# A decoder layer on one core: when VectorE divides, and in which bank the contexts are turned

## The chip, the cores and the metric

The kernel runs on 1 core of one Trainium2 chip. The metric is the device time of one execution in microseconds (us), the median of several runs. The engines: PE (TensorE, matmuls and transposes into PSUM), DVE (VectorE), ACT (ScalarE), POOL (GpSimd) and SP (SyncE, which here issues DMAs). PSUM has 8 banks of 128 x 512 f32. Engines wait for each other by semaphores alone; the kernel is written without a scheduler.

## What is computed

Four sequences of 256 tokens, 128 wide, go through three residual blocks: a windowed local attention, a cross-attention on a context of 512 rows for each sequence, and a routed mixture of 12 experts with two weight matrices each. The change touches the cross-attention (16 heads of 64):

```python
lat = layer_norm(latents, ln_lat_g, ln_lat_b)
ctx = layer_norm(context, ln_ctx_g, ln_ctx_b)
q = lat @ Wq; k, v = split(ctx @ Wkv)          # by heads
k = apply_rope(k, cos, sin)
attn = clip(einsum('bhnd,bhsd->bhns', q, k) * scale, -11, 11)
out = einsum('bhns,bhsd->bhnd', softmax(attn), v)
x = x + out.reshape(b, n, INNER) @ Wo + bo
```

Products that need more than one pass are split: an operand is kept as a rounded part (`_hi`, made by ACT) and the rest (`_lo`, made by DVE as a subtraction), and three matmuls stand for one.

## The kernel before

The span has three stretches. Up to about 61 us the local attention runs, with the first keys, values and queries of the cross-attention in its gaps. Then come 32 rounds (`for r in range(NPAIR)`), one for each pair of heads, 8 for each sequence, up to about 277 us. The experts follow, first all `W1` products, then all `W2` products.

**A round.** Each engine has its own loop over r, in a fixed order, written out by hand. In PE's round r: `scores` of pair r+1 (line 1200, two halves of 8 matmuls each, into banks 0 to 3); `unit`, one tile of values for later rounds (lines 1005 to 1007, into bank 5, `EXTRA_BANK`); `key_products` of pair r+6 (lines 1016 to 1018, bank 6, `MISC_BANK`); in even rounds `queries` (lines 1134 to 1136) of two pairs to come, into the bank of an earlier pair's output; `weigh_values` of pair r (line 1219) and `sum_weights` (line 1229), both into bank 4 or 7. In rounds named in `extras` something stands at the end, in bank 5: in rounds 3, 12 and 17 the next sequence's latents are turned (line 1112), in rounds 11, 13, 19 and 21 a finished tile is projected by `Wo` (line 1238); the projections of rounds 27 and 29 go to bank 6. Values end with round 27, keys with round 25.

**Contexts.** The normalised context of sequences 1, 2 and 3 is turned by four transposes (`turn_context`, line 979) in rounds 0, 6 and 14, ahead of that round's value unit, into bank 6. ACT reads it twice (`context_f`, lines 718 and 724: an affine copy `ctx_f`, then `ctx_hi`), DVE makes `ctx_lo` (line 1491). The keys of the same round use bank 6 too, so they wait until ACT has read it (`misc_free`).

**DVE's round** begins with `divide(r - 1)`: the reciprocal of the denominators (line 1626) and the product `o_t` (line 1630). Then come, where due, a step of the latents' normalisation (`LATENT_ROUNDS`), the two `clip`s of pair r+1 (line 1619), `key_unit`, which rotates the keys (lines 1500 and 1505), and at the round's end what `extras` or `CONTEXT_ROUND` name: `context_lo`, `latents_lo` (line 1590) or `add_projected`, which adds the projected tile to `x_sb` (line 1638, line 1641 in rounds 27 and 29). `queries(j)` waits for `ox_done`, the count of finished `o_t`, since its bank held an earlier pair.

**POOL's round** adds the halves of the clipped weights (`weights_summed`, line 573, twice; `halves_summed`, line 579) for pair r+1, then adds the two parts of a rotated key (`key_sum`, line 565), whose second part comes by DMA from SP's queue (`swap_halves`, line 348, two buffers `raw`). Ahead of the loop it adds the keys of pairs 0 to 3, then waits for the local attention's result, then adds the weights of pair 0.

**The order** around the change is set by counts: `MISC` and `EXTRA` list what goes through banks 6 and 5, and `MISC_NO` and `EXTRA_NO` give each entry the count that its reader waits for. A value unit waits for `extra_read` when the round before left something in bank 5:

```python
if extras.get(r - 1) in EXTRA_NO:
    pe.wait_ge(s["extra_read"], EXTRA_NO[extras[r - 1]] + 1)
unit(ROUND_VALUES[r])
```

Of the kernel before, what the change touches and what calls it, by code (L numbers as in the profile page):

```python
# [7 lines left out]
P = 128  # L8
# [15 lines left out]
def decoder_layer(nc, x, ctx_in, pos, a_wq, a_wk, a_wv, a_wpost, a_wrel, a_pds,  # L24
# [77 lines left out]
    with ExitStack() as ctx:  # L102
        def sb(name, shape, dt=F32, where=ctx):
            return where.enter_context(nc.sbuf_tensor(name, shape, dt))
# [36 lines left out]
        def bank(i, parts=P):  # L141
            return psum[0:parts, i, :]
# [74 lines left out]
        q_t = sb("q_t", [P, 2, QH // 2, S], F32, second)  # L217
        e_sb = sb("e_sb", [P, ERING, 2, KH, S], F32, second)
        v_sb.append(sb("v_sb1", [P, KC, HG, DX], F32, second))
        e_part = sb("e_part", [P, 2, 2, 2, S], F32, second)  # L220
        rden = sb("rden", [P, 2, S], F32, second)
# [80 lines left out]
        LATENT_ROUNDS = {1: (0, 1, 2), 2: (9, 10, 11), 3: (14, 15, 16)}  # L302
        CONTEXT_ROUND = {0: 1, PPB - 2: 2, 2 * PPB - 2: 3}
        CONTEXT_NORM = {2: 2, PPB: 3}
# [6 lines left out]
        MISC_BANK, EXTRA_BANK = 6, 5  # L311
        MISC, EXTRA = [("queries", 0)], []
        for r in range(NPAIR):
            if r in CONTEXT_ROUND:
                MISC.append(("context", CONTEXT_ROUND[r]))
            if r + K_LEAD < NPAIR:
                MISC.append(("keys", r + K_LEAD))
            if r in extras:
                (EXTRA if r < NPAIR - K_LEAD else MISC).append(extras[r])
        MISC_NO = {what: n for n, what in enumerate(MISC)}  # L320
        EXTRA_NO = {what: n for n, what in enumerate(EXTRA)}

        def key_slot(p):
# [188 lines left out]
        def _(pool):  # L512
# [91 lines left out]

            for p in range(4):
                key_sum(p)
            pool.wait_ge(s["x1_done"], NT)
            weights_summed(0)
            weights_summed(1)
            halves_summed(0)  # L610
            for r in range(NPAIR):
                for b, rounds in LATENT_ROUNDS.items():
# [37 lines left out]
        def _(act):  # L650
# [64 lines left out]
            def context_f(b):  # L715
                if b >= 1:
                    act.wait_ge(s["ctx_lo_done"], b)
                act.activation(ctx_f[:, :], bank(7 if b == 0 else MISC_BANK), ACT.Identity, scale=affine[:, 2:3], bias=affine[:, 3:4])\
                   .then_inc(s["misc_read" if b else "ctx_f_done"], 1)
                if b:  # L720
                    act.wait_ge(s["misc_read"], MISC_NO["context", b] + 1)
                else:
                    act.wait_ge(s["ctx_f_done"], 1)
                act.activation(ctx_hi[:, b % 2, :], ctx_f[:, :], ACT.Copy).then_inc(s["ctx_hi_done"], 1)
# [156 lines left out]
            exponent(1)  # L881
            outputs_turned(5)

            def context_normalize(b):
# [15 lines left out]
            for r in range(NPAIR):  # L900
                if r + 1 < NPAIR:
                    exponent(2 * r + 2)
                    exponent(2 * r + 3)
                if r in CONTEXT_ROUND:
                    misc_wait(("context", CONTEXT_ROUND[r]))
                    context_f(CONTEXT_ROUND[r])
                if r in ROUND_VALUES:
                    value_unit(ROUND_VALUES[r])
                if r % 2 == 0 and r // 2 + 1 < NQ:
                    queries_out(r // 2 + 1)  # L910
                if r in CONTEXT_NORM:
                    context_normalize(CONTEXT_NORM[r])
# [40 lines left out]
        def _(pe):  # L953
# [295 lines left out]
            turn_outputs(5)  # L1249
            local_project(2)  # L1250
            local_project(3)

# [58 lines left out]
            for r in range(NPAIR):  # L1311
# [5 lines left out]
                if r == 0:  # L1317
                    pe.wait_ge(s["x1_done"], NT)
                if r in CONTEXT_ROUND:
                    misc_free(("context", CONTEXT_ROUND[r]))  # L1320
                    turn_context(CONTEXT_ROUND[r], MISC_BANK, "misc_ps")
                if r in ROUND_VALUES:
                    route_read(2 * r - 2)
                    if extras.get(r - 1) in EXTRA_NO:
                        pe.wait_ge(s["extra_read"], EXTRA_NO[extras[r - 1]] + 1)
                    unit(ROUND_VALUES[r])
# [3 lines left out]
                if r % 2 == 0 and r // 2 + 1 < NQ:  # L1330
                    queries(r // 2 + 1)
                weigh_values(2 * r)
                route_1(2 * r)
# [93 lines left out]
        def _(dve):  # L1427
# [312 lines left out]
            local_residual(2)  # L1740
            local_residual(3)

            beside = {6: (output_bias, 0), NPAIR - 6: (output_bias, 1)}
# [6 lines left out]
            for r in range(NPAIR):  # L1750
                if r:
                    divide(r - 1)
                if r == NORM_ROUND:
                    final_norm(0, 0)
# [8 lines left out]
                if r == NORM_ROUND:  # L1763
                    final_norm(0, 1)
                if r in CONTEXT_ROUND:
                    context_lo(CONTEXT_ROUND[r])
                if r in beside:
                    work, arg = beside[r]
                    work(arg)
                route_1(2 * r)  # L1770
                if r in extras:
                    if extras[r][0] == "latents":
                        latents_lo(extras[r][1])
                    else:
                        add_projected(extras[r])
                route_1(2 * r + 1)
# [85 lines left out]
```

## Time and profile before

| | us |
|---|---|
| median of 3 runs | 430.64 (429.86 to 430.83) |
| the profiled execution | 430.4 |
| its span, first to last instruction | 428.5 |
| PE busy (share) | 402.4 (94%) |
| DVE busy | 332.6 (78%) |
| POOL busy | 260.0 (61%) |
| ACT busy | 177.8 (41%) |

The granted clock of TensorE is full in each of the 40 slices of the span. Busy shares are means over stretches with different limits; matmuls overlap in the records, so a busy PE need not be one at its peak. A row of the timeline gives the start, the duration, the engine, the line, the operation with what it writes and reads, how many instructions were merged, and in brackets how long the engine had been idle before it and what ended that idle time.

### The profile page before, as it was taken

To read this page: it belongs to the slowest core of one execution; us is meant where nothing else is said; L and a number is where in the kernel's file an instruction comes from. 1 tells how busy PE (TensorE), PEld (TensorE's weight loads), DVE (VectorE), ACT (ScalarE), POOL (GpSimd) and SP (SyncE) were. 2 spreads that over 40 slices of the span, in tenths; PEclk is the share of its full clock that TensorE was granted. 3 is DMA by queue.
4 is the path that set the end of the run, shared out by engine and by line. 5 is a ranking of instruction groups with operands and counts; after the bars stand their busy time and mean duration, and the time that the engine had idled before them with its cause. 6 is when DMAs were issued, how large, how long until landed. Compare 5 with 4: busy or idle time off the path is not lost.

```text
span 428.5 us, 8269 instructions
## 1 busy us (share of the span) xinstructions
PE 402.4 (94%) x3040; PEld 294.8 (69%) x3040; DVE 332.6 (78%) x655; ACT 177.8 (41%) x282; POOL 260.0 (61%) x225
## 2 busy tenths in 40 slices
PE   3988798989999999989999998999999999999996
PEld 2666675656677776757676675687767888888885
DVE  8888768998999978997788997886778861755544
ACT  6867354454464335443355435335257533000000
POOL 6823539999798988998979777767434850000000
PEclk9999999999999999999999999999999999999999
DMA  7696432131211111111201161547337730000000
GB/s 179 160 214 102 79 81 54 45 83 47 51 26 49 27 49 33 41 46 34 50 24 41 36 115 40 154 70 155 61 95 164 152 61 2 6 7 14 6 6 14
DMA packets 84746, 28.63 MB, mean 67 GB/s; under 512 B 71957, under 2 KB 79050, under 8 KB 84706
## 3 DMA queue, kind: packets, MB, share of 16 engines
q1 hardware_dynamic: 81748, 26.80, 28.3%
q10 hardware_dynamic: 2958, 1.30, 1.3%
q8 instruction: 25, 0.41, 0.4%
q14 instruction: 15, 0.12, 0.1%
HBM read 17.67 MB, written 2.02 MB: 46 GB/s over the span
## 4 chain that ended last, share of the span: by engine, by line
PE 66%; DVE 16%; SPq 7%; issue 4%; ACT 2%; DMA 2%; POOL 2%; DVEq 0%; ACTq 0%; POOLq 0%
PE psum L1219 10%; PE psum L1200 9%; PE psum L1402 5%; PE psum L1403 5%; PE psum L1401 5%; SPq L415 5%; PE psum L1362 4%; PE psum L1364 4%; PE psum L1363 4%; DVE rden L1626 4%; PE psum L1238 3%; PE psum L1229 3%; DVE e_sb L1619 2%; PE psum L1005 2%; PE psum L972 1%
## 5 line engine op out<-in xcount | busy, mean ns | idle before, releaser
L573 POOL TENSOR_TENSOR e_part<-e_sb 128x512 f32<-128x512 f32 x64 | 90.6, 1434 | 20.4 <-DVE e_sb L1619 20.4
L830 ACT ACTIVATE e_sb<-psum 128x1024 f32<-128x1024 f32 x64 | 62.2, 1022 | 85.0 <-PE psum L1200 82.9
L1200 PE MATMUL psum<-q_t,kT 64*128 64x256 f32 x512 | 64.2, 389 | 0.0
L1219 PE MATMUL psum<-e_sb,v_sb 128*64 128x256 f32 x512 | 63.8, 386 | 0.0
L1626 DVE RECIPROCAL rden<-psum 128x256 f32<-128x256 f32 x32 | 55.9, 1748 | 9.6 <-PE psum L1229 9.4
L1826 DVE SCALAR_TENSOR_TENSOR x_sb<-psum,dw,x_sb 128x128 f32<-128x128 f32 x96 | 33.7, 351 | 38.1 <-PE psum L1403 35.5
L1619 DVE TENSOR_SCALAR e_sb<-e_sb 128x1024 f32<-128x1024 f32 x64 | 58.6, 948 | 2.8 <-ACT e_sb L830 2.6
L1200 PEld LDWEIGHTS psum<-q_t,kT 64*128 64x128 f32 x512 | 46.7, 186 | 13.9 <-issue 8.4
L1219 PEld LDWEIGHTS psum<-e_sb,v_sb 128*64 128x64 f32 x512 | 33.7, 136 | 22.3 <-issue 6.3
L565 POOL TENSOR_TENSOR kT<-kT,raw 128x512 f32<-128x512 f32 x32 | 44.1, 1377 | 8.1 <-DMA raw<-rope_b 8.1
L602 POOL TENSOR_TENSOR xeT_lo<-xeT,xeT_hi 128x512 fp32r<-128x512 f32 x24 | 31.4, 1309 | 28.4 <-ACT xeT_hi L844 28.3
L579 POOL TENSOR_TENSOR e_part<-e_part 128x512 f32<-128x512 f32 x32 | 41.8, 1306 | 2.5
L1362 PE MATMUL psum<-xeT_hi,w1T_hi 128*128 128x512 f32 x96 | 38.9, 405 | 0.8 <-ACT h_f L946 0.5
L1402 PE MATMUL psum<-w2T_lo,h_hi 128*128 128x512 f32 x96 | 38.0, 396 | 0.0
L1403 PE MATMUL psum<-w2T_hi,h_lo 128*128 128x512 f32 x96 | 37.8, 394 | 0.0
L1364 PE MATMUL psum<-xeT_hi,w1T_lo 128*128 128x512 f32 x96 | 37.5, 391 | 0.0
L1363 PE MATMUL psum<-xeT_lo,w1T_hi 128*128 128x512 f32 x96 | 37.5, 390 | 0.0
L1401 PE MATMUL psum<-w2T_hi,h_hi 128*128 128x512 f32 x96 | 37.3, 389 | 0.0
L844 ACT ACTIVATE xeT_hi<-xeT 128x512 fp32r<-128x512 f32 x24 | 15.2, 632 | 29.4 <-DVE xeT L1669 21.3
L1362 PEld LDWEIGHTS psum<-xeT_hi,w1T_hi 128*128 128x128 f32 x96 | 18.0, 188 | 7.0 <-issue 2.6
L1500 DVE TENSOR_TENSOR rope_b<-psum,sinT 128x512 f32<-128x512 f32 x30 | 20.4, 679 | 2.1 <-PE psum L1018 2.1
L1505 DVE TENSOR_TENSOR kT<-psum,cosT 128x512 f32<-128x512 f32 x32 | 21.6, 676 | 0.0
(202 smaller groups left out, 729.9 us busy)
## 6 DMA issues: line engine op xcount, KB each, us to landing
raw<-rope_b SPq DMA_DIRECT2D x116, 64.0 KB, 2.0
w_raw<-in_L_ffn_W_dram SPq DMA_DIRECT2D x96, 64.0 KB, 2.3
gates<-gate_dram SPq DMA_DIRECT2D x6, 768.0 KB, 4.4
ctx_sb<-in_ctx_dram SPq DMA_DIRECT2D x4, 256.0 KB, 6.1
vbd<-v_dram SPq DMA_DIRECT2D x16, 52.6 KB
v_dram<-v_tok SPq DMA_DIRECT2D x4, 136.0 KB
raw<-in_L_xattn_Wkv_dram SPq DMA_DIRECT2D x2, 256.0 KB, 5.7
kT<-in_L_xattn_Wkv_dram SPq DMA_DIRECT2D x2, 256.0 KB, 4.7
```

The costliest lines, as they stand in the source:

```text
L573: pool.tensor_tensor(e_part[:, p % 2, half, :, :], e_sb[:, i % ERING, :, 0, :], e_sb[:, i % ERING, :, 1, :], ALU.add)\
L830: act.activation(e_sb[:, i % ERING, :, :, :].rearrange("p a k t -> p (a k t)"), psum[:, a:a + 2, :].rearrange("p a b -> p (a b)"), ACT.Exp ...
L1200: mm = pe.matmul(psum[:, 2 * (i % 2) + a, t * S:(t + 1) * S], key_slot(p)[rows, kt * P:(kt + 1) * P], q_t[rows, j % 2, p % 2, :], start=Tr ...
L1219: mm = pe.matmul(psum[DX * a:DX * a + DX, pv_bank(p), 0:S], v_sb[g % 2][:, kt, 2 * pp + a, :], e_sb[:, i % ERING, a, t, :], start=(kt == 0 ...
L1362: pe.matmul(bank(c), w1T_hi[:, e, c, :], hi, start=(e == 0), stop=False)
L1363: pe.matmul(bank(c), w1T_hi[:, e, c, :], lo, start=False, stop=False)
L1364: mm = pe.matmul(bank(c), w1T_lo[:, e, c, :], hi, start=False, stop=(e == NE - 1))
L1401: pe.matmul(o, hi, w_hi, start=(c == 0), stop=False)
L1402: pe.matmul(o, hi, w_lo, start=False, stop=False)
L1403: mm = pe.matmul(o, lo, w_hi, start=False, stop=(c == HC - 1))
L1619: dve.tensor_scalar(e, e, E_LO, E_HI, ALU.max, ALU.min).then_inc(s["clip_done"], 1)
L1626: dve.reciprocal(rden[:, p % 2, :], psum[:, pv_bank(p), S:2 * S]).then_inc(s["rden_done"], 1)
```

## The change

It has these parts. The second context (sequence 1) is turned ahead of the loop, between the last two local projections, into bank 6; ACT reads it after the last `outputs_turned`, DVE makes its rest after the last local residual. Contexts 2 and 3 are turned in rounds 6 and 14 into bank 5, behind keys and queries, once the round's values have been read; ACT reads them after `queries_out`, and DVE makes their rest a round later, in rounds 7 and 15. The latents' rest is made a round later, in rounds 4, 13 and 18. The projected tiles of rounds 11, 13, 19, 21 and 27 are added a round later, right behind the division. POOL adds the weights of pair 0 between the keys of pairs 1, 2 and 3; its wait for the whole local attention is replaced by one for the first sequence's normalised latents, ahead of the first key, and `e_part` changes places with `v_sb1` in SBUF.

```diff
         e_sb = sb("e_sb", [P, ERING, 2, KH, S], F32, second)
+        e_part = sb("e_part", [P, 2, 2, 2, S], F32, second)
         v_sb.append(sb("v_sb1", [P, KC, HG, DX], F32, second))
-        e_part = sb("e_part", [P, 2, 2, 2, S], F32, second)
...
-        CONTEXT_ROUND = {0: 1, PPB - 2: 2, 2 * PPB - 2: 3}
+        CONTEXT_ROUND = {PPB - 2: 2, 2 * PPB - 2: 3}
...
-        MISC, EXTRA = [("queries", 0)], []
+        MISC, EXTRA = [("queries", 0), ("context", 1)], []
         for r in range(NPAIR):
             if r in CONTEXT_ROUND:
-                MISC.append(("context", CONTEXT_ROUND[r]))
+                EXTRA.append(("context", CONTEXT_ROUND[r]))
...
+        def extra_before(r):
+
+            at = [EXTRA_NO[what] for q in range(r) for what in (("context", CONTEXT_ROUND.get(q)), extras.get(q)) if what in EXTRA_NO]
+            return max(at, default=-1) + 1
...
-            for p in range(4):
-                key_sum(p)
-            pool.wait_ge(s["x1_done"], NT)
+            pool.wait_ge(s["lat_in_done"], TPB)
+            key_sum(0)
+            key_sum(1)
             weights_summed(0)
+            key_sum(2)
             weights_summed(1)
             halves_summed(0)
+            key_sum(3)
...
             outputs_turned(5)
+            misc_wait(("context", 1))
+            context_f(1)
...
-                if r in CONTEXT_ROUND:
-                    misc_wait(("context", CONTEXT_ROUND[r]))
-                    context_f(CONTEXT_ROUND[r])
                 if r in ROUND_VALUES:
                     value_unit(ROUND_VALUES[r])
                 if r % 2 == 0 and r // 2 + 1 < NQ:
                     queries_out(r // 2 + 1)
+                if r in CONTEXT_ROUND:
+                    act.wait_ge(s["extra_ps"], EXTRA_NO["context", CONTEXT_ROUND[r]] + 1)
+                    context_f(CONTEXT_ROUND[r])
...
             local_project(2)
+            turn_context(1, MISC_BANK, "misc_ps")
             local_project(3)
...
-                if r in CONTEXT_ROUND:
-                    misc_free(("context", CONTEXT_ROUND[r]))
-                    turn_context(CONTEXT_ROUND[r], MISC_BANK, "misc_ps")
                 if r in ROUND_VALUES:
                     route_read(2 * r - 2)
-                    if extras.get(r - 1) in EXTRA_NO:
-                        pe.wait_ge(s["extra_read"], EXTRA_NO[extras[r - 1]] + 1)
+                    if extra_before(r) > extra_before(r - 1):
+                        pe.wait_ge(s["extra_read"], extra_before(r))
                     unit(ROUND_VALUES[r])
...
                     queries(r // 2 + 1)
+                if r in CONTEXT_ROUND:
+                    pe.wait_ge(s["v_done"], r + V_LEAD + 1)
+                    turn_context(CONTEXT_ROUND[r], EXTRA_BANK, "extra_ps")
                 weigh_values(2 * r)
...
             local_residual(3)
+            context_lo(1)
...
                     divide(r - 1)
+                if extras.get(r - 1, "none")[0] == "project" and r - 1 < NPAIR - 3:
+                    add_projected(extras[r - 1])
...
-                if r in CONTEXT_ROUND:
-                    context_lo(CONTEXT_ROUND[r])
+                if r - 1 in CONTEXT_ROUND:
+                    context_lo(CONTEXT_ROUND[r - 1])
...
-                if r in extras:
-                    if extras[r][0] == "latents":
-                        latents_lo(extras[r][1])
-                    else:
-                        add_projected(extras[r])
+                if extras.get(r - 1, "none")[0] == "latents":
+                    latents_lo(extras[r - 1][1])
+                if r in extras and r >= NPAIR - 3:
+                    add_projected(extras[r])
```

## Rows read from the trace of the kernel before

**Rows 1.** The page: the chain that ended last, share by engine.
```profile
PE 66%; DVE 16%; SPq 7%; issue 4%; ACT 2%; DMA 2%; POOL 2%; DVEq 0%; ACTq 0%; POOLq 0%
```
**Rows 2.** Timeline of PE: where rounds 0, 1, 4 to 9 begin.
```profile
61.50 2.00 PE L1200 MATMUL psum<-q_t,kT 64*128 64x256 f32 x16
...
70.48 2.00 PE L1200 MATMUL psum<-q_t,kT 64*128 64x256 f32 x16
...
89.91 2.00 PE L1200 MATMUL psum<-q_t,kT 64*128 64x256 f32 x16
...
98.08 2.00 PE L1200 MATMUL psum<-q_t,kT 64*128 64x256 f32 x16
...
103.90 2.00 PE L1200 MATMUL psum<-q_t,kT 64*128 64x256 f32 x16
...
111.66 2.00 PE L1200 MATMUL psum<-q_t,kT 64*128 64x256 f32 x16
...
117.48 2.00 PE L1200 MATMUL psum<-q_t,kT 64*128 64x256 f32 x16
...
124.02 2.00 PE L1200 MATMUL psum<-q_t,kT 64*128 64x256 f32 x16
```
**Rows 3.** Timeline of PE: its gaps, and one context's transposes (PEld).
```profile
60.85 0.71 PE L1105 MATMUL psum<-awT,oT 128*128 128x128 f32 x4 [0.45 <-ACT oT L761]
...
69.90 0.65 PE L1229 MATMUL psum<-e_part,ones 128*64 128x256 f32 x4 [1.00 <-POOL e_part L579]
...
80.54 0.35 PE L1134 MATMUL psum<-lat_hi,wq_hi 128*128 128x256 f32 x1 [0.64 <-DVE o_t L1630]
...
94.90 0.35 PE L1134 MATMUL psum<-lat_hi,wq_hi 128*128 128x256 f32 x1 [1.40 <-DVE o_t L1630]
...
105.83 0.42 PEld L979 LDWEIGHTS psum<-ident,ctx_sb 128*128 128x128 f32 x4 [0.33 <-issue]
...
162.75 0.50 PE L1016 MATMUL psum<-ctx_hi,wkv_hi 128*128 128x512 f32 x1 [0.56 <-ACT ctx_f L718]
...
189.94 0.36 PE L1134 MATMUL psum<-lat_hi,wq_hi 128*128 128x256 f32 x1 [1.16 <-DVE o_t L1630]
```
**Rows 4.** Busy times of a stretch; DVE's lat_lo (ns, min/median/max); DVE's timeline there.
```profile
70.50:95.00 24.50, 22.46 (x159) 15.17 (x158) 24.20 (x30) 12.83 (x19) 23.33 (x19) 1.00 0.23 60
...
L1590 DVE TENSOR_TENSOR lat_lo<-lat_f,lat_hi x4: 426/1250/1528, 53.6 to 186.4; 128x256 fp32r<-128x256 f32 x4
...
91.10 1.53 DVE L1590 TENSOR_TENSOR lat_lo<-lat_f,lat_hi 128x256 fp32r<-128x256 f32 x1
...
94.33 0.42 DVE L1630 TENSOR_TENSOR o_t<-psum,rden 128x256 f32<-128x256 f32 x1
```
**Rows 5.** Timeline of POOL and of SP's queue around round 0 and in round 4.
```profile
61.36 1.27 POOL L565 TENSOR_TENSOR kT<-kT,raw 128x512 f32<-128x512 f32 x1 [2.70 <-DMA raw<-rope_b]
...
68.23 2.42 SPq L348 DMA_DIRECT2D raw<-wo_sb  x4
...
89.39 2.96 POOL L573 TENSOR_TENSOR e_part<-e_sb 128x512 f32<-128x512 f32 x2
```
**Rows 6.** DVE's four additions of projected tiles and their waits; round 12's start.
```profile
L1638 DVE TENSOR_TENSOR x_sb<-psum,x_sb x4: 274/292/292, 144.6 to 215.4; 128x128 f32<-128x128 f32 x4
...
  PE psum L1238: 6.3, 3
...
144.79 1.74 DVE L1626 RECIPROCAL rden<-psum 128x256 f32<-128x256 f32 x1
...
146.12 0.50 PE L1005 MATMUL psum<-wkv_hi,ctx_hi 128*128 128x512 f32 x1
```
**Rows 7.** DVE's last context rest, round 16's division, PE's queries behind it.
```profile
164.95 0.97 DVE L1491 TENSOR_TENSOR ctx_lo<-ctx_f,ctx_hi 128x512 fp32r<-128x512 f32 x1
...
174.85 0.42 DVE L1630 TENSOR_TENSOR o_t<-psum,rden 128x256 f32<-128x256 f32 x1
...
175.90 0.28 PE L1134 MATMUL psum<-lat_hi,wq_hi 128*128 128x256 f32 x1
```

More of the change, by code:

```diff
@@ L717, in context_f @@
                     act.wait_ge(s["ctx_lo_done"], b)
-                act.activation(ctx_f[:, :], bank(7 if b == 0 else MISC_BANK), ACT.Identity, scale=affine[:, 2:3], bias=affine[:, 3:4])\
-                   .then_inc(s["misc_read" if b else "ctx_f_done"], 1)
-                if b:
+                act.activation(ctx_f[:, :], bank((7, MISC_BANK, EXTRA_BANK, EXTRA_BANK)[b]), ACT.Identity, scale=affine[:, 2:3], bias=affine[:, 3:4])\
+                   .then_inc(s[("ctx_f_done", "misc_read", "extra_read", "extra_read")[b]], 1)
+                if b >= 2:
+                    act.wait_ge(s["extra_read"], EXTRA_NO["context", b] + 1)
+                elif b:
                     act.wait_ge(s["misc_read"], MISC_NO["context", b] + 1)
```

## The prediction

> **What bounds the kernel now.** I read the chain of waits first: two thirds of the span hang on PE, a sixth on DVE [rows 1]. So a change pays where PE stands still, and I listed PE's matmuls in order of time through the 32 attention rounds. The reader is to see two things. A round has a price of its own: an odd round costs 103.90 - 98.08 = 5.82, an even one, which also makes queries, 124.02 - 117.48 = 6.54 [rows 2]. And PE's gaps are few and all named [rows 3]: a context being read out of its bank (162.75; the same in rounds 0 and 6), POOL's sum of the weights (69.90), and the queries waiting for a division's result o_t (80.54, 94.90, 189.94). A gap costs some 0.2 more than its length: round 4 takes 98.08 - 89.91 = 8.17, 1.63 over an even round, with a gap of 1.40; I add 0.2 to each further gap. Last I read DVE and POOL beside these gaps, to see what either was doing then. From 70.5 to 95 DVE is busy for 24.20 of 24.50 us and POOL for 23.33 [rows 4]: there PE is paced by them, and what PE gains there must also fit into them.
>
> **Part 1: the second context ahead of the loop, POOL's new order.** Round 0 takes 70.48 - 61.50 = 8.98 [rows 2], 2.44 over an even round. In it PE turns the context, waits until ACT has read it before the keys may use the bank, and then waits 1.00 for POOL's sums [rows 3]. Before the loop the four transposes (0.42 of weight loads at 105.83) fall into the 0.45 that PE waits for oT ahead of the last local projection [rows 3]; I price them at nothing, and at 0.42 if that gap closes. ACT reads the context there while it would wait for the first scores of round 0; DVE's rest ctx_lo leaves round 0, so the first division can follow PE's sums as early as these come.
> POOL now adds the first halves of the weights while it waits for the third pair's key transfer (its idle 2.70 before 61.36 [rows 5]), so the sums no longer come last in round 0. The third addition is not delayed, as its transfer lands at 61.36 anyway; the fourth comes some 3 us later than now. SP's fifth swap waits for it, but is issued at 68.23 behind five small loads [rows 5], and its scores come in round 2, not before 61.50 + 6.54 + 5.82 = 73.9. The new wait of POOL's first addition stands where nothing is in a hurry: nothing.
> So PE gains 2.4 in round 0. Not all of it lasts: DVE and POOL have no idle time to run faster in rounds 1 to 3 [rows 4]. When a DVE operation meets a POOL one, it waits: the four lat_lo last 0.43 at the shortest and 1.25 in the median [rows 4]; the one at 91.10 ends 0.28 after POOL's pair of additions does (89.39 + 2.96) [rows 4, 5]. I give back one such wait, 1.25 - 0.43 = 0.8, and for the range none or two. Term: 1.6 (0.8 to 2.4).
> The Trainium skill (SBUF — State Buffer, section "Who interferes with whom") says that a DVE instruction with two SBUF inputs and a GpSimd instruction that reads SBUF exclude each other for a whole instruction; the row at 91.10 agrees. By that rule each moved rest is as dear in its new place as a POOL addition standing there, and it speaks against counting any of them as hidden.
>
> **Part 2: rests a round later.** Division already comes first in DVE's round (line 1752); what changes is what stands right ahead of it, at the end of the round before.
> Round 4: lat_lo takes DVE from 91.10 to 92.63, the division follows without a gap, o_t ends at 94.75, and PE's queries, ready 1.40 earlier, begin at 94.90 [rows 3, 4]. Without lat_lo there o_t comes 1.5 sooner; the gap goes. Late next is the rest itself, behind round 4's key rotation; it pushes that division by up to 1.5, but the next query waits for a later one. Term: 1.4, between 0 (DVE late anyway) and 1.6.
> Rounds 11, 13, 19, 21 end in a projection, and DVE's addition of it to x_sb now stands behind the next division. PE's next value unit needs that bank. In three of the four DVE now idles for PE's projection, 6.3 us in all [rows 6]; the division fits in there, free. The fourth is round 11: DVE is late, adds at once, and divides at 144.79. With the division first from 144.6, the addition ends after 1.74 + 0.42 + 0.29 = 2.45, at 147.05, but the value unit begins at 146.12 [rows 4, 6]: PE waits 0.93, with the refill 1.1. Term: -1.1 (0 if DVE comes a microsecond sooner, as it may, since the rounds before are moved about; -1.3 if a little later).
>
> **Part 3: contexts 2 and 3 in the values' bank.** In rounds 6 and 14 the keys no longer wait for ACT's read; the gap of 0.56 goes [rows 3]. Round 6 takes 111.66 - 103.90 = 7.76, which is 0.8 over an even round with its 0.42 of transposes [rows 2, 3]; the transposes stay. The new wait for the values' read stands behind keys and queries, of which the queries alone take 6.54 - 5.82 = 0.72, and ACT has read by then unless it is late: nothing, at most 0.4. The next value unit waits for the context's read, a whole half-round away: nothing. Round 6: 0.8 (0.4 to 0.8).
> Round 14 gains the same 0.8, but the rest of context 3, 0.97 now at 164.95, goes behind round 15, where DVE has two normalisations more. There the division is already without slack: its o_t begins at 174.85, ends at 175.27, and PE's queries need it at 175.90 [rows 7]. 0.97 is 0.34 more than the 0.63 between them: PE waits 0.34, with refill 0.6. Round 18 loses its 1.16 gap [rows 3], 1.4 with the refill, as lat_lo leaves; DVE carries some 0.4 of the rest into it, so I count 1.0. Together 0.8 - 0.6 + 1.0 = 1.2 (0 to 2.2).
>
> **Sum.** 1.6 + 1.4 + 0.8 - 1.1 + 1.2 = 3.9 us. The profiled execution took 430.4 (span 428.5); it becomes 426.5. The median of the runs shown, 430.64, lies 0.24 above it and becomes 426.7. Behind round 25 all work is set off by PE or by what PE set off, and every load there waits for a count of such work, so I let the gain run to the end; the addition of round 27, moved too, I take at nothing.
>
> **Rivals.**
> All of it lands: no port wait is given back, DVE is in time in rounds 12 and 16. Then 2.4 + 1.6 + 0.8 + 0.8 + 1.4 = 7.0: 423.6. For it: each gap goes by its cause. Against: DVE's late start at 144.79 and the short slack at 175.27.
> The early rounds stay as long as DVE and POOL need. Then part 1 keeps 0.8 and round 4's gap only changes its owner: 3.9 - 0.8 - 1.4 = 1.7, or 428.9. For it: 24.20 of 24.50 [rows 4]. Against: lat_lo is 1.5 of these 24.20, and it leaves ahead of the division that counts. This is what the skill's rule above would do here, if POOL's additions stand where DVE's operations come.
> The division-first order does nothing, because DVE waits for PE's denominators as before: rounds 4 and 18 keep their gaps, 3.9 - 1.4 - 1.0 = 1.5, or 429.1. Against: lat_lo ends where the division begins [rows 4].
> Slower, by the values' bank: all four projections are added too late, as in round 11. If the division starts L before the next value unit, PE waits 2.45 - L, four times. Everything else brings 5.0, so it turns at 4 x (2.45 - L) = 5.0, L = 1.2; round 11 has 1.5. At L = 0.5 it costs 7.8: 2.8 slower, 433.4. Against: the 6.3 idle in the other three.
>
> **How the numbers follow.** Forecast 0.50; all lands 0.19; early rounds bound 0.19; order idle 0.05; bank late 0.07. A measurement tells 0.2% (0.86 us) from nothing, so faster means under 429.8: the first two, and most of the third and fourth (0.17 of 0.24), 0.86; same 0.07, the rest of these; slower 0.07. The range runs from the case where all lands, 423.6, to just past the two small-gain cases, 429.2; it leaves out the bank's case, half of the first rival and what lies over the small cases, 0.2 together. Of the signs, faster holds nearly all, so one range does.
>
> **What would show it.** Right: round 0 at 6.5 us and no wait for POOL in it; no PE gap ahead of the queries of round 4 and a small one or none in 18; no gap ahead of the keys in rounds 6 and 14; a new gap of about 0.9 ahead of round 12's value unit, and one of 0.3 ahead of round 16's queries. Wrong: rounds 1 to 3 longer than 5.82 + 6.54 + 5.82 and the present 0.64 + 0.2 of round 2 by over 0.8; gaps ahead of the value units of rounds 14, 20 and 22; lat_lo still ending where a division that PE waits for begins.

## Result, and the profile after

The changed kernel takes 426.76 us (median of 4 runs, 426.47 to 427.39) where the kernel before took 430.74 beside it: a ratio of 0.990, with a 95% interval of 0.985 to 0.994. The profiled execution took 426.81, its span 424.9 against 428.5. The forecast was 426.7. The time came out; one step behind it did not.

The page of the kernel after: busy times, the granted clock in 40 slices, the chain that ended last.

```profile
PE 402.7 (95%) x3040; PEld 296.0 (70%) x3040; DVE 336.0 (79%) x655; ACT 178.2 (42%) x282; POOL 257.5 (61%) x225
...
PEclk9999989999999999999999999999999999999999
...
PE 58%; DVE 31%; issue 4%; ACT 2%; DMA 2%; ACTq 1%; POOL 0%; DVEq 0%
```

DVE has 31% of the chain where it had 16% [rows 1]: more of the end now hangs on VectorE. POOL and SP's queue have left it. Where that is, PE's timeline says. The rows below are the starts of rounds (L1211 is L1200 of before) and every gap of PE ahead of a round's work that the text speaks of; the bracket holds the idle time and what ended it.

```profile
62.16 2.00 PE L1211 MATMUL psum<-q_t,kT 64*128 64x256 f32 x16
68.67 2.00 PE L1211 MATMUL psum<-q_t,kT 64*128 64x256 f32 x16
...
78.97 0.36 PE L1145 MATMUL psum<-lat_hi,wq_hi 128*128 128x256 f32 x1 [0.88 <-DVE o_t L1642]
...
88.36 2.00 PE L1211 MATMUL psum<-q_t,kT 64*128 64x256 f32 x16
...
95.23 2.00 PE L1211 MATMUL psum<-q_t,kT 64*128 64x256 f32 x16
...
113.85 2.00 PE L1211 MATMUL psum<-q_t,kT 64*128 64x256 f32 x16
...
118.34 0.35 PE L1145 MATMUL psum<-lat_hi,wq_hi 128*128 128x256 f32 x1 [0.91 <-DVE o_t L1642]
...
121.53 2.00 PE L1211 MATMUL psum<-q_t,kT 64*128 64x256 f32 x16
...
144.36 0.50 PE L1016 MATMUL psum<-wkv_hi,ctx_hi 128*128 128x512 f32 x1 [0.67 <-DVE x_sb L1650]
...
173.85 0.35 PE L1145 MATMUL psum<-lat_hi,wq_hi 128*128 128x256 f32 x1 [0.32 <-DVE o_t L1642]
...
256.43 0.35 PE L1145 MATMUL psum<-lat_hi,wq_hi 128*128 128x256 f32 x1 [1.26 <-DVE o_t L1642]
```

A round's length is the difference of two such starts; round 0 is now 68.67 - 62.16 = 6.51, against 8.98. The table holds the rounds that differ by over 0.03 us between its four kernels; the others repeat within that in all twelve profiles, except round 26 in one (told below). Round 4 also moves by itself: in six profiles of kernels that are alike up to it, it takes from 6.72 to 6.88. The column "three moves" is a version found on the way, "and the bias" the last one.

| round | before | after | three moves | and the bias | what ended a gap there, after |
|---|---|---|---|---|---|
| 0 | 8.98 | 6.51 | 6.53 | 6.54 | |
| 2 | 7.41 | 7.66 | 7.64 | 7.68 | o_t, 0.88 |
| 4 | 8.17 | 6.87 | 6.88 | 6.88 | |
| 6 | 7.76 | 6.97 | 6.97 | 6.98 | |
| 8 | 6.54 | 7.68 | 6.53 | 6.53 | o_t, 0.91, new |
| 12 | 6.91 | 7.64 | 6.90 | 6.93 | projected add, 0.67, new |
| 14 | 7.76 | 6.97 | 6.97 | 6.97 | |
| 16 | 6.53 | 7.08 | 6.53 | 6.54 | o_t, 0.32, new |
| 18 | 7.93 | 6.53 | 6.53 | 6.52 | |
| 28 | 7.33 | 7.13 | 7.13 | 5.83 | o_t, 1.26 |

After minus before, the ten rounds come to -2.47 + 0.25 - 1.30 - 0.79 + 1.14 + 0.73 - 0.79 + 0.55 - 1.40 - 0.20 = -4.28. Round 0 began at 62.16 and not at 61.50: +0.66. Together -3.62, the difference of the profiled times (430.4 to 426.8). In this execution, and not in that of the kernel before, TensorE's granted clock fell for a while ahead of the loop (last section).

Round 8 is the surprise. VectorE's timeline in the kernel after shows how it comes about (a bracket would hold its idle time; the first rows have none):

```profile
95.67 1.52 DVE L1602 TENSOR_TENSOR lat_lo<-lat_f,lat_hi 128x256 fp32r<-128x256 f32 x1
97.11 1.75 DVE L1638 RECIPROCAL rden<-psum 128x256 f32<-128x256 f32 x1
...
107.82 1.79 DVE L1597 TENSOR_TENSOR x_sb<-x_sb,bo_all 128x512 f32<-128x512 f32 x1
109.54 1.75 DVE L1638 RECIPROCAL rden<-psum 128x256 f32<-128x256 f32 x1
...
114.28 1.79 DVE L1503 TENSOR_TENSOR ctx_lo<-ctx_f,ctx_hi 128x512 fp32r<-128x512 f32 x1
115.99 1.75 DVE L1638 RECIPROCAL rden<-psum 128x256 f32<-128x256 f32 x1
117.77 0.42 DVE L1642 TENSOR_TENSOR o_t<-psum,rden 128x256 f32<-128x256 f32 x1
...
121.64 1.76 DVE L1638 RECIPROCAL rden<-psum 128x256 f32<-128x256 f32 x1 [0.84 <-PE psum L1240]
```

The first idle time of VectorE since the loop's beginning is the 0.84 ahead of 121.64. So lat_lo, moved behind round 4's division to 95.67, delays the division of round 5; no query waits for that one, but the lateness is handed on through the bias (107.82) and the rest of context 2, which now stands at 114.28, to the division at 115.99, for which the queries of round 8 do wait. The stretch as a whole shows why nothing absorbed it. Rounds 0 to 7 before and after (length, then busy time of PE, PEld, DVE, ACT, POOL, granted clock, DMA share, GB/s):

```profile
61.50:117.48 55.98, 51.82 (x371) 34.84 (x371) 51.46 (x66) 26.95 (x38) 50.11 (x39) 1.00 0.23 57
...
62.16:113.85 51.69, 50.71 (x368) 34.71 (x367) 51.28 (x66) 26.44 (x38) 48.37 (x37) 1.00 0.22 55
```

VectorE is busy for nearly the same time in both. Before, it was idle for 55.98 - 51.46 = 4.52 us of these rounds; PE's earlier arrival leaves it 51.69 - 51.28 = 0.41. Was it lat_lo, ctx_lo, or GpSimd, beside which 1.79 was measured? That is what the experiments had to tell.

### The profile page after: what moved, and what is told of

It is laid out like the page before. It is cut to its first block, busy times and chain, and to the rows that moved or that the text cites. A ratio compares the mean times of both kernels' runs of the same rounds, so it can differ in the third digit from the quotient of the medians.

```text
span 424.9 us, 8269 instructions
## 1 busy us (share of the span) xinstructions
PE 402.7 (95%) x3040; PEld 296.0 (70%) x3040; DVE 336.0 (79%) x655; ACT 178.2 (42%) x282; POOL 257.5 (61%) x225
## 4 chain that ended last, share of the span: by engine, by line
PE 58%; DVE 31%; issue 4%; ACT 2%; DMA 2%; ACTq 1%; POOL 0%; DVEq 0%
PE psum L1230 7%; DVE rden L1638 7%; PE psum L1211 6%; DVE e_sb L1631 6%; PE psum L1414 5%; PE psum L1415 5%; PE psum L1413 5%; PE psum L1374 4%; PE psum L1376 4%; PE psum L1375 4%; PE psum L1249 3%; PE psum L1240 2%; DVE rope_b L1512 2%; DVE xn L1457 2%; DVE kT L1517 2%
## 5 line engine op out<-in xcount | busy, mean ns | idle before, releaser
L578 POOL TENSOR_TENSOR e_part<-e_sb 128x512 f32<-128x512 f32 x64 | 88.4, 1397 | 25.7 <-DVE e_sb L1631 25.7
L1631 DVE TENSOR_SCALAR e_sb<-e_sb 128x1024 f32<-128x1024 f32 x64 | 63.8, 1026 | 5.9 <-ACT e_sb L839 5.9
L1211 PE MATMUL psum<-q_t,kT 64*128 64x256 f32 x512 | 64.2, 389 | 0.0
L1230 PE MATMUL psum<-e_sb,v_sb 128*64 128x256 f32 x512 | 63.8, 386 | 0.0
L1211 PEld LDWEIGHTS psum<-q_t,kT 64*128 64x128 f32 x512 | 46.7, 186 | 13.9 <-issue 8.4
L1661 DVE STREAM_TRANSPOSE psum<-w_raw 128x512 f32<-128x512 f32 x24 | 17.4, 726 | 4.8 <-DMA w_raw<-in_L_ffn_W_dram 2.8
```

The costliest lines, as they stand in the source:

```text
L578: pool.tensor_tensor(e_part[:, p % 2, half, :, :], e_sb[:, i % ERING, :, 0, :], e_sb[:, i % ERING, :, 1, :], ALU.add)\
L1211: mm = pe.matmul(psum[:, 2 * (i % 2) + a, t * S:(t + 1) * S], key_slot(p)[rows, kt * P:(kt + 1) * P], q_t[rows, j % 2, p % 2, :], start=Tr ...
L1230: mm = pe.matmul(psum[DX * a:DX * a + DX, pv_bank(p), 0:S], v_sb[g % 2][:, kt, 2 * pp + a, :], e_sb[:, i % ERING, a, t, :], start=(kt == 0 ...
L1631: dve.tensor_scalar(e, e, E_LO, E_HI, ALU.max, ALU.min).then_inc(s["clip_done"], 1)
```

## The experiments

**The two halves of part 1, and both.** On the kernel before: GpSimd's order alone; the second context ahead of the loop alone; both.

```diff
-        v_sb.append(sb("v_sb1", [P, KC, HG, DX], F32, second))
         e_part = sb("e_part", [P, 2, 2, 2, S], F32, second)
+        v_sb.append(sb("v_sb1", [P, KC, HG, DX], F32, second))
...
-            for p in range(4):
-                key_sum(p)
-            pool.wait_ge(s["x1_done"], NT)
+            pool.wait_ge(s["lat_in_done"], TPB)
+            key_sum(0)
+            key_sum(1)
             weights_summed(0)
+            key_sum(2)
             weights_summed(1)
             halves_summed(0)
+            key_sum(3)
```

```diff
-        CONTEXT_ROUND = {0: 1, PPB - 2: 2, 2 * PPB - 2: 3}
+        CONTEXT_ROUND = {PPB - 2: 2, 2 * PPB - 2: 3}
...
-        MISC, EXTRA = [("queries", 0)], []
+        MISC, EXTRA = [("queries", 0), ("context", 1)], []
...
             outputs_turned(5)
+            misc_wait(("context", 1))
+            context_f(1)
...
             local_project(2)
+            turn_context(1, MISC_BANK, "misc_ps")
             local_project(3)
...
             local_residual(3)
+            context_lo(1)
```

> The kernel before with POOL's new order alone (first weights between the keys of pairs 1, 2 and 3, with the new place of e_part and the new wait); contexts and rests as before. Theory: round 0 of the kernel before loses to two things one after the other, the context's read and POOL's late sums (gap 1.00). With the sums early, round 0 should look like round 6 of the kernel before, 7.76 us in place of 8.98: 1.2 us faster, and no gap ahead of the sum of round 0. Rival (POOL's sums are late only because DVE's context rest makes the clips late): round 0 stays within 0.3 of 8.98, no gain.

> The kernel before with the second context turned, read and its rest made ahead of the loop; POOL's order as before, contexts 2 and 3 as before. Theory: POOL's sums of round 0 still end where they do now, so PE waits for them about 1 us longer than now and round 0 stays within 0.3 us of 8.98: no gain, 430.5. Rival (the context's read is what round 0 loses): round 0 falls to 7.3 to 7.8, 1.2 to 1.7 us faster.

> Both of these on the kernel before, and nothing else of the change. Theory: round 0 takes 6.5 us and round 2 some 0.25 more than before, 2.2 us faster in all, 428.5; more than the two parts added, since each alone leaves the other's wait. Rival (DVE and POOL are full in rounds 1 to 3 and take the gain back): under 1 us faster.

Measured: 429.25 (ratio 0.997, 0.995 to 1.000), 429.28 (0.998, 0.995 to 1.001) and 428.13 (0.994, 0.992 to 0.996). Round 0 is 7.74, 7.00 and 6.54. PE's timeline in round 0, with GpSimd's order alone:

```profile
65.42 0.49 PE L1018 MATMUL psum<-ctx_hi,wkv_hi 128*128 128x512 f32 x1 [0.55 <-ACT ctx_f L720]
```

and with the context ahead alone:

```profile
70.12 0.65 PE L1231 MATMUL psum<-e_part,ones 128*64 128x256 f32 x4 [0.24 <-POOL e_part L579]
```

With the order alone, GpSimd's gap is gone and the context's remains, as expected. With the context ahead alone, the expectation of a nearly unchanged round 0 missed in the length. In that profile round 0 began at 63.7, 2.2 later than before (it is one of those with a fall of TensorE's clock, last section), and PE got GpSimd's sum at 70.12 against 69.90 [rows 3]: nearly the same time, though PE's part had begun so much later. That fits a sum which GpSimd's own queue of work sets, but it is one profile with a late start, and the interval of the ratio reaches from a gain of half a per cent to none; what this half brings alone stays open. Both together shorten round 0 by 2.44 and lengthen round 2 by 0.24 and round 4 by 0.15: 2.05 net. Part 1 thus gives back some 0.25 to waits, or 0.4 if round 4's 0.15 counts, by which that round also moves without any edit; not the 0.8 that I took.

**The latents' rest in its old place.** The kernel after, with lat_lo at the end of its own round, ahead of the division.

```diff
-                if extras.get(r - 1, "none")[0] == "latents":
-                    latents_lo(extras[r - 1][1])
+                if extras.get(r, "none")[0] == "latents":
+                    latents_lo(extras[r][1])
```

> The changed kernel with the latents' rest back at the end of the round in which the latents are turned; all else as changed. Theory: lat_lo again stands right ahead of the divisions that the queries of rounds 4 and 18 wait for: gaps of 1.0 to 1.4 there, rounds of 8.0 us in place of 6.87 and 6.53, 2.5 us slower than the changed kernel, 429.3. Rival (the division waits for PE's denominators whatever stands ahead of it): under 0.5 us slower.

Measured: 428.14 (0.994, 0.991 to 0.997), only 1.4 more than the kernel after. PE's timeline, rounds 4 and 18, then VectorE's:

```profile
93.15 0.36 PE L1145 MATMUL psum<-lat_hi,wq_hi 128*128 128x256 f32 x1 [1.56 <-DVE o_t L1642]
...
187.88 0.36 PE L1145 MATMUL psum<-lat_hi,wq_hi 128*128 128x256 f32 x1 [0.69 <-DVE o_t L1642]
```

```profile
96.45 1.76 DVE L1638 RECIPROCAL rden<-psum 128x256 f32<-128x256 f32 x1 [0.86 <-PE psum L1240]
...
115.91 1.75 DVE L1638 RECIPROCAL rden<-psum 128x256 f32<-128x256 f32 x1
```

Round 4 is 8.33 again and round 18 is 7.45, so the order counts there. Round 16 grew as well, 7.49 for 7.08: VectorE's normalisation at 166.36 took 1.00 us there, beside a key addition of GpSimd, and 0.59 in the kernel after, so its next division came later. But round 8 is 6.53, without a gap. VectorE catches up: it idles 0.86 ahead of the division after round 4's, which it did not after the change. Its division of round 8 begins at 115.91, in the kernel after at 115.99 (54.11 and 53.83 from the start of round 0): nearly the same time, while PE comes to round 8 at 114.97 here and at 113.85 there. So of the 8.33 - 6.87 = 1.46 that the move gains in round 4, 7.68 - 6.53 = 1.15 is given back in round 8. VectorE needs its time up to there either way: in rounds 0 to 7 it is busy for 51.31 us here and for 51.28 in the kernel after.

**The rest of context 2 one round later; the addition of round 11 in its own round; the rest of context 3 one round earlier.** Three single edits of the kernel after, in this order.

```diff
-                if r - 1 in CONTEXT_ROUND:
-                    context_lo(CONTEXT_ROUND[r - 1])
+                if r in {8: 2, 15: 3}:
+                    context_lo({8: 2, 15: 3}[r])
...
-                if extras.get(r - 1, "none")[0] == "project" and r - 1 < NPAIR - 3:
+                if extras.get(r - 1, "none")[0] == "project" and r - 1 < NPAIR - 3 and r - 1 != PPB + 3:
                     add_projected(extras[r - 1])
...
-                if r in extras and r >= NPAIR - 3:
+                if r in extras and (r >= NPAIR - 3 or r == PPB + 3):
                     add_projected(extras[r])
...
-                if r - 1 in CONTEXT_ROUND:
-                    context_lo(CONTEXT_ROUND[r - 1])
+                if r in {7: 2, 14: 3}:
+                    context_lo({7: 2, 14: 3}[r])
```

> The changed kernel with the rest of context 2 made in round 8 in place of round 7. Theory: the new gap ahead of round 8's queries (0.91, round 8 at 7.68 us) comes from this rest, which follows the output bias of round 6 with DVE already late; in round 8 it stands ahead of a division that no query waits for in the round after. Round 8 goes back to 6.54, rounds 9 and 10 stay at 5.82 and 6.54: 1.1 us faster than the changed kernel, 425.6. Rival (DVE is simply full from round 1 on, so the wait only moves): round 10 takes over 1 us more, no gain.

> The changed kernel with the projection of round 11 added at the end of round 11 again, the others a round later as changed. Theory: DVE is late there and adds at once, so the gap of 0.67 ahead of round 12's value unit goes and round 12 takes 6.91 as in the kernel before: 0.7 us faster, 426.0. Rival (the bank is read late because the value unit itself comes early now): round 12 stays at 7.6.

> The changed kernel with the rest of context 3 made in round 14, behind its keys, in place of round 15. Theory: DVE has about 1 us idle there ahead of the next division, so it costs nothing, and the gap ahead of round 16's queries (0.32, round 16 at 7.08) goes: 0.5 us faster, 426.2. Rival (ACT reads the context too late in round 14 and DVE waits for it ahead of the division): round 16 no shorter, or round 15 longer, no gain or up to 0.5 slower.

Measured: 425.56 (0.988, 0.983 to 0.993), 425.73 (0.988, 0.983 to 0.993) and 426.29 (0.990, 0.987 to 0.993); the intervals don't tell these from the kernel after, so the rounds have to. First edit: round 8 falls from 7.68 to 6.52, and rounds 9 and 10 stay, so the gap needs ctx_lo in front of that division. It needs the late lat_lo as well: in the experiment before this one ctx_lo stood in the same place, with lat_lo early, and there was no gap. But the lateness travels once more, with no idle row of VectorE on the way, to round 12 (8.07 for 7.64), where the value unit waits longer for the addition:

```profile
144.85 0.50 PE L1016 MATMUL psum<-wkv_hi,ctx_hi 128*128 128x512 f32 x1 [1.10 <-DVE x_sb L1650]
```

Second: round 12 falls from 7.64 to 6.90, its length before the change, and nothing behind it moves; that addition was better where it had been. Third: round 16 falls from 7.08 to 6.58, but round 18 rises from 6.53 to 6.87, a net gain of 0.16. No o_t gap is marked in either, but the queries of round 18 begin 0.15 after o_t ends, as they do in each marked wait for it (94.90 after 94.75 in the kernel before), so they still wait a little:

```profile
184.44 0.42 DVE L1642 TENSOR_TENSOR o_t<-psum,rden 128x256 f32<-128x256 f32 x1
...
185.01 0.36 PE L1145 MATMUL psum<-lat_hi,wq_hi 128*128 128x256 f32 x1
```

VectorE is late there by its clips of round 16, which took 2.37 us beside a key addition of GpSimd and 1.28 in the kernel after; from them to round 18 it has no idle row.

**The three together.** The edit below, beside the second one above.

```diff
-                if r - 1 in CONTEXT_ROUND:
-                    context_lo(CONTEXT_ROUND[r - 1])
+                if r in {8: 2, 14: 3}:
+                    context_lo({8: 2, 14: 3}[r])
```

> The three moves together on the changed kernel. Theory: the gaps are in different rounds, so their gains add: 1.1 + 0.7 + 0.5 = 2.3 us faster than the changed kernel, 424.4, a ratio to the kernel before of about 0.985. Rival (DVE is the bound of the stretch and carries the work on): under 1 us faster than the changed kernel.

Measured: 423.89 (0.984, 0.980 to 0.988). Rounds 8, 12, 16 and 18 all stand at 6.53 to 6.90, with none of the trades seen in the single edits. Against the kernel after that is 1.15 + 0.74 + 0.55 = 2.44 by the rounds.

**GpSimd's share.** The kernel after, in which GpSimd's additions of weights take one column from the third pair on.

```diff
+                cols = slice(0, S if p < 2 else 1)
-                pool.tensor_tensor(e_part[:, p % 2, half, :, :], e_sb[:, i % ERING, :, 0, :], e_sb[:, i % ERING, :, 1, :], ALU.add)\
+                pool.tensor_tensor(e_part[:, p % 2, half, :, cols], e_sb[:, i % ERING, :, 0, cols], e_sb[:, i % ERING, :, 1, cols], ALU.add)\
...
+                cols = slice(0, S if p < 2 else 1)
-                pool.tensor_tensor(e_part[:, p % 2, 0, :, :], e_part[:, p % 2, 0, :, :], e_part[:, p % 2, 1, :, :], ALU.add)\
+                pool.tensor_tensor(e_part[:, p % 2, 0, :, cols], e_part[:, p % 2, 0, :, cols], e_part[:, p % 2, 1, :, cols], ALU.add)\
```

> The changed kernel, in which GpSimd sums only the first column of each row of weights from the third pair on; the rest of the sum of the weights is left out, so the denominators of those pairs are not the softmax's. GpSimd's 2.9 and 1.6 us additions shrink to fixed costs of some tenths of a us. Theory: VectorE's one-pass operations (ctx_lo and the projected adds at 1.8 us, lat_lo at 1.5) are long because they wait for GpSimd's additions to end, and this is what leaves VectorE late in rounds 2, 8, 12 and 16. Then these rounds shrink to about 6.5 to 6.9 us each (from 7.66, 7.68, 7.64 and 7.08), lat_lo to 0.5 us and ctx_lo to about 0.7 us, and the time falls by 3 to 3.8 us to about 423. Rival: VectorE's own work, the weights' rests above all, fills the rounds whatever GpSimd does; then rounds 2 and 8 keep their 7.66 and 7.68 us, and the time stays within 1 us of the changed kernel's 426.8.

Measured: 421.32 (0.979, 0.975 to 0.982), below the theory's 423. The page, VectorE's and GpSimd's timelines, and the groups of VectorE's lines (busy us, mean ns, then idle time ahead), of this kernel:

```profile
PE 400.3 (96%) x3040; PEld 295.2 (71%) x3040; DVE 310.0 (74%) x655; ACT 177.8 (43%) x282; POOL 152.7 (36%) x225
...
PE 80%; DVE 12%; ACT 2%; issue 2%; DMA 2%; ACTq 1%; POOL 0%; DVEq 0%
```

```profile
L1633 DVE TENSOR_SCALAR e_sb<-e_sb 128x1024 f32<-128x1024 f32 x64 | 46.1, 734 | 12.4 <-ACT e_sb L841 12.3
```

```profile
110.60 1.22 DVE L1505 TENSOR_TENSOR ctx_lo<-ctx_f,ctx_hi 128x512 fp32r<-128x512 f32 x1
...
165.79 0.68 DVE L1505 TENSOR_TENSOR ctx_lo<-ctx_f,ctx_hi 128x512 fp32r<-128x512 f32 x1
```

```profile
109.99 1.27 POOL L570 TENSOR_TENSOR kT<-kT,raw 128x512 f32<-128x512 f32 x1
```

and, for comparison, the same group and GpSimd's additions around the two long rests in the kernel after:

```profile
L1631 DVE TENSOR_SCALAR e_sb<-e_sb 128x1024 f32<-128x1024 f32 x64 | 63.8, 1026 | 5.9 <-ACT e_sb L839 5.9
```

```profile
93.96 2.95 POOL L578 TENSOR_TENSOR e_part<-e_sb 128x512 f32<-128x512 f32 x2
...
112.64 2.88 POOL L578 TENSOR_TENSOR e_part<-e_sb 128x512 f32<-128x512 f32 x2 [0.63 <-DVE e_sb L1631]
```

Rounds 4, 8, 12 and 16 fall to 6.53, 6.53, 6.90 and 6.54, round 26 from 6.28 to 5.93 and round 28 from 7.13 to 5.83: 0.34 + 1.15 + 0.74 + 0.54 + 0.35 + 1.30 = 4.42; the rest of the span's fall of 6.5 is round 0's start, at 60.08 for 62.16. In the chain VectorE has 12% for the 31% after the change. It has the same 655 instructions and is busy 336.0 - 310.0 = 26.0 us less, so that much of its busy time goes with GpSimd's additions: by the rows, it was waiting for them. 63.8 - 46.1 = 17.7 of it lies in the clips of the weights (the expectation calls them rests): 1026 ns in the mean, 734 now. The theory had put it on the rests and the projected adds (what it calls an add of 1.8 us is the output's bias; a projected add takes 0.28); it named the right engine and the smaller part of the bill. lat_lo fell to 0.95 us in the loop, not to 0.5. In the kernel after, lat_lo ends at 95.67 + 1.52 = 97.19, 0.28 after GpSimd's pair of additions (93.96 + 2.95 = 96.91), and ctx_lo at 116.07, 0.55 after (115.52). With those gone, ctx_lo lasts 0.68 when only one-column additions stand beside it and 1.22 when the key addition does (109.99 to 111.26, it ends at 111.82).

The Trainium skill (SBUF — State Buffer, section "Who interferes with whom") adds to its rule on two SBUF inputs that a tensor_scalar in a two-port mode excludes GpSimd too, whoever issues first holding the ports for a whole instruction. The clips have one input and stay in SBUF; at their shortest they take 0.66 us for 1024 elements, where ctx_lo takes 0.68 for 512, so they run at twice its pace. Their fall from 1026 to 734 ns agrees with the rule; that the ports are what they wait for, no run here shows by itself.

Round 2 kept its 7.68 and a gap of 0.91, which by the expectation speaks for the rival there. It doesn't settle it: the experiment left the additions of pairs 0 and 1 whole, and one of these still ran beside round 1's normalisation. What holds round 2 stays open. That GpSimd itself being early, and not the free ports, shortened the other rounds is not excluded by this run alone; against it, each gap that went had been ended by o_t or x_sb, VectorE's results, and VectorE's idle time ahead of its divisions rose from 9.1 us (after) to 22.6 (this kernel):

```profile
L1638 DVE RECIPROCAL rden<-psum 128x256 f32<-128x256 f32 x32 | 55.9, 1747 | 9.1 <-PE psum L1240 9.1
...
L1640 DVE RECIPROCAL rden<-psum 128x256 f32<-128x256 f32 x32 | 56.1, 1754 | 22.6 <-PE psum L1242 22.5
```

**The bias in an idle round.** The three moves, and the second half of the output's bias in round 20. In the kernel after it stands in round 26:

```profile
243.83 1.77 DVE L1597 TENSOR_TENSOR x_sb<-x_sb,bo_all 128x512 f32<-128x512 f32 x1
```

```diff
-            beside = {6: (output_bias, 0), NPAIR - 6: (output_bias, 1)}
+            beside = {6: (output_bias, 0), 20: (output_bias, 1)}
```

> The version with three moves, in which the second half of the output's bias is added in round 20 and not in round 26. Theory: the gaps ahead of the queries of rounds 26 and 28 (0.17 and 1.26 us) are there because VectorE is late by this addition of 1.76 us; in round 20 it idles, so the addition costs nothing there, both gaps go, round 28 falls from 7.13 to 6.5 us or a little less than that, the two together give up to 1.4 us, and the time falls from 423.9 to about 422.5. Rival: the gap of round 28 is set by the division and what stands ahead of it in rounds 27 and 28 themselves, not by round 26; then round 28 keeps 7.13 us and the time stays within 0.3 us of 423.9, or rises by what rounds 21 and 22 pay.

Measured: 423.02 (0.982, 0.979 to 0.986). Round 28 falls from 7.13 to 5.83, so its gap is gone, and rounds 20 to 22 keep their lengths: the addition is free there. Round 26 keeps 6.26 and its small gap, so the theory was wrong on that one: the bias stood behind round 26's own division (o_t ended at 242.71 in the kernel after). PE's timeline, the last gaps ahead of queries:

```profile
80.38 0.36 PE L1145 MATMUL psum<-lat_hi,wq_hi 128*128 128x256 f32 x1 [0.91 <-DVE o_t L1642]
...
241.87 0.35 PE L1145 MATMUL psum<-lat_hi,wq_hi 128*128 128x256 f32 x1 [0.17 <-DVE o_t L1642]
```

By rounds 8, 12, 16 and 28 this version is 1.15 + 0.71 + 0.54 + 1.30 = 3.70 us shorter than the kernel after; by the medians, 426.76 - 423.02 = 3.7. The two weren't timed beside each other, and their intervals against the kernel before just touch (0.985 to 0.994 and 0.979 to 0.986); it is the rounds that show the order.

## Why the prediction was right, and where it was not

The time was right because the misses cancelled. Point by point:

- **Part 1, 1.6.** Measured 2.47 in round 0 less 0.25 in round 2, 2.2; alone, 2.05. The mechanism held, and the wait given back, taken as 0.8, was 0.25, or 0.4 with round 4's 0.15. The order alone leaves the context's gap, as it should; how much of the rest the context brings by itself is not settled.
- **Round 4, 1.4.** Measured 1.30; the gap is no longer marked. A little of it is left: the round still takes 0.34 over 6.53, which went with GpSimd's additions. The step that failed stands right behind it: "it pushes that division by up to 1.5, but the next query waits for a later one". I priced the lateness as ending at the next division. Rows 4 had VectorE busy for 24.20 of 24.50 us, and I did not ask when it would next be idle. In the kernel before it had 4.5 us of idle time in rounds 0 to 7, and the terms for PE in these rounds, 4.3 by what was measured, used up nearly all of it. In the kernel after it was idle not until 120.8 (0.84 ahead of 121.64), after the rest of context 2 had come on top, which I had also put at nothing. The queries of round 8 paid 1.14. This is my second rival, "the early rounds stay as long as DVE and POOL need", in part: it had the gap changing its owner, and it did, for 1.15 of 1.46.
- **Round 6, 0.8, and round 14, 0.8.** Measured 0.79 and 0.79: the keys no longer wait for a context to be read out of their bank, and the new wait for the values costs nothing.
- **The projections' additions, -1.1.** Round 12 rose by 0.73, with a gap of 0.67 for the forecast's 0.93; the other three cost nothing, as said. The edit that puts this one addition back takes the 0.74 away, so the cause is shown. The rival that all four come late did not happen.
- **Rounds 16 and 18, -0.6 and +1.0.** Round 16 rose by 0.55, with a gap of 0.32 for the 0.34 that was worked out. That match is luck in part: the rest, taken as 0.97, lasted 1.51 there (at 170.07), and the normalisation ahead of it 0.59 for 1.07. Round 18 fell by 1.40 and not by 1.0: I let VectorE carry 0.4 of the rest into it, and its o_t ended at 185.89, 0.75 ahead of the queries. With round 14 the three make 1.64 for 1.2.
- **Round 28.** The late addition of round 27, "at nothing", brought 0.20: it used to stand ahead of a division that the queries of round 28 wait for (at 257.47, the division at 257.67). No run moves this addition alone.
- **A gap left out.** The prediction calls PE's gaps "few and all named", but the longest in the 32 rounds of the kernel before is not in its rows, and the 1.30 that the bias gave later lay there:

```profile
260.01 0.36 PE L1134 MATMUL psum<-lat_hi,wq_hi 128*128 128x256 f32 x1 [1.46 <-DVE o_t L1630]
```

So the sum was too low by 0.6 for part 1, 0.4 for round 12, 0.4 for rounds 14 to 18 and 0.2 for round 28, and too high by 0.1 for round 4 and 1.14 for round 8: 4.28 in the rounds for 3.9. Round 0's later start took 0.66 of that in the profiled execution. The edits ahead of the loop don't force that: both halves of part 1 without the others began round 0 at 60.6, earlier than the 61.50 of before.

## What to carry to other kernels

On an engine that has no idle time, work moved behind the urgent instruction is late for the next urgent one: follow its timeline to the next idle row before calling the move free, and add up all that is moved into that stretch. Each microsecond that PE gains is one less in which the engine beside it may idle. Put such work ahead of a division that nobody waits for, or where the engine idles; two moves of that kind and one addition put back gave 2.4 us more here, and a bias moved into an idle round another 1.3. Where the stretch ahead of a loop varies by more than the effect, compare the lengths of the rounds, which repeated within 0.03 us (round 4 within 0.16), and not spans.

## What the hardware showed that I had not expected

Working beside GpSimd's additions of weights costs VectorE some 26 us of its 336.0 busy ones here, and most of it hides in an instruction with one input, the clip, not in the subtractions that I watched. The change itself made the clips dearer, by 5.2 us, which no term of the sum has. They took 63.8 us after it and before it:

```profile
L1619 DVE TENSOR_SCALAR e_sb<-e_sb 128x1024 f32<-128x1024 f32 x64 | 58.6, 948 | 2.8 <-ACT e_sb L830 2.6
```

The start of round 0 varied from 60.1 to 63.7 us over the twelve profiles, though the instructions ahead of it hardly differ. In four of the ten versions and in the kernel after, TensorE's granted clock fell to 0.50, its lower level of 1.2 GHz, for some us ahead of the loop. The windows of the kernel after (length, busy time of PE, PEld, DVE, ACT, POOL, granted clock, DMA share, GB/s):

```profile
50.00:52.00 2.00, 1.12 (x6) 0.80 (x6) 1.79 (x6) 0.33 (x1) 1.09 (x3) 1.00 0.58 123
52.00:54.00 2.00, 1.94 (x9) 1.50 (x9) 0.86 (x4) 1.20 (x3) 1.12 (x1) 0.64 0.36 93
54.00:56.00 2.00, 2.00 (x30) 1.78 (x33) 0.84 (x5) 1.10 (x2) 0.99 (x1) 0.50 0.42 102
```

and of the kernel before:

```profile
50.00:52.00 2.00, 0.77 (x5) 0.61 (x5) 1.75 (x8) 0.33 (x1) 1.08 (x3) 1.00 0.52 109
52.00:54.00 2.00, 1.68 (x9) 1.06 (x9) 0.86 (x5) 1.48 (x4) 1.18 (x1) 1.00 0.40 74
54.00:56.00 2.00, 1.93 (x69) 1.80 (x70) 1.18 (x7) 0.92 (x2) 0.00 (x0) 1.00 0.42 108
```

PE was busy for 1.12 of the 2 us ahead of the fall in the one, and for 0.77 in the other, where the clock did not fall. What decides it these runs don't show. In the five profiles with such a fall round 0 began at 61.6, 62.2, 63.3, 63.5 and 63.7, in the seven without at 60.1 to 61.8.
